# First attention of a fused decoder: weight splits on GpSimd, norms spread over the steps, a drain with its own order

## The reference, cut to what matters

```python
x = x + L0_attn(layernorm(x), wq, bq, wk, bk, wv, bv, wo, bo, ln_g, ln_b)
# inside: residual = h; h is normalised again, x = ln(h) * ln_g + ln_b
# q, k, v = x @ w.T + b, 16 heads of 128; rope(q), rope(k)
# attn = softmax(causal(q k' / sqrt(128))); o = attn v; return o @ wo.T + bo + residual
x = x + L0_xattn(layernorm(x), ctx, ctx, Wh, ...)     # V = einsum('bshd,hde->bshe', ctx, Wh)
```

## Time and profile before

| what | value |
|---|---|
| median of 3 runs | 999.65 us |
| profiled execution, its own time | 1000.2 us |
| its span | 998.4 us |
| TensorE busy over the span | 936.3 us (94%) |
| VectorE, ScalarE busy | 795.0 us (80%), 709.2 us (71%) |
| GpSimd busy | 359.3 us (36%) |
| mean granted TensorE clock | 0.99 |

### The profile page before, as it was taken

The page is one execution under the profiler, slowest core; times in us unless marked ns, Lnnn a source line. Parts: engine busy times, 40 slices in busy tenths (PEclk is TensorE's granted clock), DMA queues, the critical chain, the costliest instruction groups (busy, mean ns, idle before and its releaser), DMA issues. The chain is left out here.

```text
span 998.4 us, 19509 instructions
## 1 busy us (share of the span) xinstructions
PE 936.3 (94%) x6587; PEld 780.0 (78%) x6603; DVE 795.0 (80%) x1558; ACT 709.2 (71%) x1973; POOL 359.3 (36%) x323
## 2 busy tenths in 40 slices
PE   8789999999999999999969988788999989999998
PEld 4678888888889888898968876667778789875554
DVE  5999988888878797888827889889999754476885
ACT  5878877888778887777732347599999735448882
POOL 2343333433434334433300120166655310006882
PEclk9999999999999999999999997999999999999999
DMA  6423000000000000200125000000000000008762
GB/s 212 122 79 88 21 24 24 25 23 23 24 23 24 24 22 25 59 23 24 47 80 141 1 1 1 1 2 2 2 2 2 2 1 2 1 27 279 239 221 85
DMA packets 62084, 50.58 MB, mean 51 GB/s; under 512 B 18273, under 2 KB 53537, under 8 KB 61985
## 3 DMA queue, kind: packets, MB, share of 16 engines
q1 hardware_dynamic: 61984, 49.34, 16.7%
HBM read 36.74 MB, written 2.23 MB: 39 GB/s over the span
## 5 line engine op out<-in xcount | busy, mean ns | idle before, releaser
L391 POOL TENSOR_TENSOR roped_q<-roped_q,sin_q 128x512 f32<-128x512 f32 x64 | 82.9, 1295 | 261.9 <-DVE sin_q L553 261.9
L459 ACT ACTIVATE P<-banks,neg_max 128x128 f32<-128x128 f32 x256 | 90.4, 368 | 26.4 <-DVE neg_max L571 25.8
L391 POOL TENSOR_TENSOR roped_k<-roped_k,sin_k 128x512 f32<-128x512 f32 x64 | 82.9, 1296 | 45.5 <-DVE sin_k L553 45.5
L1745 ACT ACTIVATE win_P<-banks,win_neg_max 128x128 f32<-128x128 f32 x256 | 91.0, 382 | 4.9 <-DVE win_neg_max L1832 4.3
L499 ACT ACTIVATE oT_hi<-banks,bv_col 128x512 fp32r<-128x512 f32 x64 | 43.9, 687 | 67.5 <-PE banks L727 67.5
L1678 POOL TENSOR_TENSOR win_P<-win_P,win_inv 128x512 f32<-128x512 f32 x64 | 66.5, 1040 | 52.7 <-DVE win_inv L1837 52.6
L468 ACT ACTIVATE sin_q<-banks 64x512 f32<-64x512 f32 x128 | 75.9, 593 | 3.4 <-PE banks L37 1.1
L468 ACT ACTIVATE sin_k<-banks 64x512 f32<-64x512 f32 x128 | 75.8, 592 | 3.0 <-PE banks L37 0.8
L698 PE MATMUL banks<-roped_k,roped_q 128*128 128x128 f32 x512 | 68.3, 277 | 8.1 <-ACT banks L449 8.1
L683 PE MATMUL banks<-WO_lo,oT_hi 128*128 128x256 f32 x256 | 73.3, 286 | 2.4 <-DVE oT_lo L574 2.3
L552 DVE SCALAR_TENSOR_TENSOR roped_k<-banks,qk_bias,cos 128x512 f32<-128x512 f32 x64 | 48.0, 750 | 30.6 <-ACT sin_k L468 30.3
(11 more groups left out here) (439 smaller groups left out, 3093.0 us busy)
## 6 DMA issues: line engine op xcount, KB each, us to landing
PT<-blocks SPq DMA_DIRECT2D x630, 16.0 KB, 1.8
ret_V<-moe_gate_rows SPq DMA_DIRECT2D x16, 512.0 KB, 4.8
ctx<-moe_gate_rows SPq DMA_DIRECT2D x16, 512.0 KB, 5.5
X<-in_x SPq DMA_DIRECT2D x4, 512.0 KB, 6.8
stage<-in_wqT SPq DMA_DIRECT2D x4, 512.0 KB, 4.0
stage<-in_wvT SPq DMA_DIRECT2D x4, 512.0 KB, 6.6
stage<-in_woT SPq DMA_DIRECT2D x4, 512.0 KB, 4.9
ctx<-in_ctxT SPq DMA_DIRECT2D x4, 512.0 KB, 4.5
```

Source lines behind the costliest of these rows:

```text
L391: nc.gpsimd.tensor_tensor(roped[w][:, p, :], roped[w][:, p, :], sin_part[w][:], ALU.add).then_inc(roped_sum[w], 1)
L459: ins = nc.scalar.activation(P[:, :, i, :], SC[:, i * 128:(i + 1) * 128].rearrange("p (q n) -> p q n", n=Q), ACT.Exp, bias=neg_max[:, r % ...
L1745: ins = nc.scalar.activation(P[:, h % 2, s, i, :], SC[2 * (h % 2) + s][:, i * 128:(i + 1) * 128], ACT.Exp, bias=neg_max[:, h % 2, at:at + ...
```

## The change

VectorE no longer splits the weight items 4 to 15; GpSimd does, after its adds of step t, for the items of step t+1. The statistics of batches 4 to 15 move from steps 3 to 5 to six pairs in steps 3, 4, 16, 17, 21 and 23, and the one norm of 12 batches becomes three of 4 batches at the ends of steps 5, 18 and 25, each with its powers on GpSimd. The context tiles are loaded at SyncE's steps 53, 57, 61 and 63. The four last steps become a written sequence `drain()` per engine: the last two heads (62 and 63) are transposed on TensorE, the value products use three banks, and ScalarE and VectorE take them out in turn.

```diff
-        RET_BANKS = V_, XB, QK[0], QK[1]
+        RET_BANKS = V_, XB, QK[1]
+        STATS_AT = {3: (4, 5), 4: (6, 7), HEADS0: (8, 9), HEADS0 + 1: (10, 11), HEADS0 + 5: (12, 13), HEADS0 + 7: (14, 15)}
+        NORMS_AT = {5: 1, HEADS0 + 2: 2, HEADS0 + 9: 3}
+        POWERS_AT = NORMS_AT
-        LAST = STEPS - 1
+        LAST = STEPS - 2
+        LAST_BANKS = QK[0], SC
+        CTX_AT = {STEPS - 11: 0, STEPS - 7: 1, STEPS - 3: 2, STEPS - 1: 3}
...
                 def load_ctx(g):
-                    if g == 0:
-                        sp.wait_ge(v_projected, NG * HEADS0)
+                    sp.wait_ge(v_projected, (NG - 1) * HEADS0 + 4 * g + 4)
...
+                def split_weights(i):                      # GpSimd
+                    src, hi, lo = parts(i)
+                    pool.wait_ge(weights_rounded, i + 1)
+                    pool.wait_ge(weights_split, i)
+                    nc.gpsimd.tensor_tensor(lo, src, hi.bitcast(F32), ALU.subtract).then_inc(weights_split, 1)
...
                 for t in range(STEPS):
                     step(t, t % 2)
+                    if t + 1 < HEADS0:
+                        for i in split_at(t + 1):
+                            split_weights(i)
...
-                    if t == 6:
-                        powers(1)
+                    if t in POWERS_AT:
+                        powers(POWERS_AT[t])
...
+                def drain():                               # ScalarE
+                    exps(LAST)
+                    lay_mask(LAST)
+                    take_ret_V(0)
+                    take_PT(LAST)
+                    round_oT(LAST - 1)
+                    exps(LAST + 1)
+                    take_ret_V(2)
+                    round_oT(LAST)
+                    take_PT(LAST + 1)
+                    take_ret_V(4)
+                    take_ret_V(6)
+                    round_oT(LAST + 1)
...
-                    if g == 0 and r > 0:                   # VectorE
-                        for i in split_at(r):
-                            split_weights(i)
...
-                        if r in (3, 4, 5):
-                            group_stats(r - 2)
-                        if r == 6:
-                            both_norms(1)
...
+                    if s in STATS_AT:
+                        some_stats(STATS_AT[s])
+                    if s in NORMS_AT:
+                        both_norms(NORMS_AT[s])
...
+                def drain():                               # VectorE
+                    find_max(LAST)
+                    split_oT(LAST - 2)
+                    scale_last(LAST)
+                    take_ret_V(1)
+                    find_max(LAST + 1)
+                    split_oT(LAST - 1)
+                    scale_last(LAST + 1)
+                    take_ret_V(3)
+                    split_oT(LAST)
+                    take_ret_V(5)
+                    split_oT(LAST + 1)
+                    take_ret_V(7)
...
+                def drain():                               # TensorE
+                    last = lambda u: (u, u % HEADS0)
+                    retention_values(0)
+                    retention_values(1)
+                    out_project(*last(LAST - 2), NG - 1)
+                    score(LAST + 1, (LAST + 1) % 2)
+                    transpose_last(LAST)
+                    weigh(*last(LAST - 1))
+                    retention_values(2)
+                    retention_values(3)
+                    weigh(*last(LAST))
+                    out_project(*last(LAST - 1), NG - 1)
+                    transpose_last(LAST + 1)
+                    retention_values(4)
+                    weigh(*last(LAST + 1))
+                    out_project(*last(LAST), NG - 1)
+                    for p in (5, 6, 7):
+                        retention_values(p)
+                    out_project(*last(LAST + 1), NG - 1)
```

## The result

Six runs of the changed kernel have a median of 1004.2 us (1002.25 to 1005.92), six of the kernel before 999.56: the ratio is 1.0049, with a 95% interval of 1.0032 to 1.0066. The change costs half a per cent. The profiled execution took 1004.77 us by its own time, its span is 1002.7 (998.4 before).

What follows compares the result with a forecast made beforehand. VectorE and ScalarE's loop was taken to bound group 0, TensorE group 1, context waits the drain. +6.6 + 5.2 - 5.9 = +5.9 us on the median 999.65 gave 1005.5 us; range 995 to 1010, likeliest case alone 1002 to 1009.

Steps and rivals of the forecast that it cites:

- group 0: Steps 0 to 15: GpSimd's splits and the moved norm make TensorE start step 16 later by 6.6 us.
- group 1: From step 16: statistics and norms moved here make rounds exceed TensorE's steps, costing 5.2 us.
- the drain: Last four steps: context waits and half-clock value matmuls go, less new waits; gain 5.9 us.
- Collision: Group 0: GpSimd's 1024-column split shuts out VectorE's scaling until it ends; rounds 8.3 us, 8.7 with a batch; chance 0.58.
- Step 3: Group 0: two GpSimd splits, over the scaling and the q sine product, cost 2.1, less 1.2 and 0.67: +0.2 us.
- The norm's trap: Step 5: the norm's last two-input operation waits out GpSimd's split, +2.3 us, with 0 as the other end.
- The clock: Step 5: TensorE's clock may fall after idling some 4.5 us, adding 0 to 2 us outside the sum.
- bare round: Time between row maxima without added VectorE work: 7.14 us, winning back only 0.23 us a step.
- lateness: Row maximum's start minus TensorE's step start; beyond 1.53 us TensorE waits; forecast 1.3 at step 16.
- the rival that it gives nothing: Drain: the new order has its own waits and its gain is gone; 1011 us, chance 0.05.
- No collision: Group 0: GpSimd's split doesn't hold the scaling, and group 0 gains 4.3 us; 994 us in all, chance 0.27.
- Half a collision: Engines share the port at half speed, or the norm slips through; 999 to 1002 us, chance 0.10.

Runs made afterwards that it cites:

- halves: The changed kernel with each GpSimd weight split made as two instructions of 512 columns; 1001.49 us, ratio 1.0021.
- drain_gpsimd: The changed kernel with statistics and the one norm of 12 batches back in their old places, GpSimd still splitting; 1000.87 us, ratio 1.0005.
- drain_only: The kernel before with only the new drain and early context loads; splits on VectorE, statistics and norm in their old places; 992.24 us, ratio 0.9935.
- drain_spread: The changed kernel with the weight splits back on VectorE, statistics and norms still spread; 994.54 us, ratio 0.9955.
- extra1024: drain_only plus one useless GpSimd subtract of 1024 columns behind the k add in each of steps 16 to 59; 1044.61 us, ratio 1.0438.
- extra512: drain_only plus one useless GpSimd subtract of 512 columns behind the k add in each of steps 16 to 59; 1000.42 us, ratio 1.0003.
- extra256: drain_only plus one useless GpSimd subtract of 256 columns behind the k add in each of steps 16 to 59; 995.83 us, ratio 0.9963.
- beside: drain_only with the statistics and norms spread, but placed behind the output's low half, beside ScalarE's exponentials; 990.79 us, ratio 0.9908.

## Why the prediction was right

The forecast was 1005.5, the median is 1004.2, and the sign came from the mechanism that was named. No errors cancelled between the three terms: group 0 cost 5.9 for 6.6, group 1 4.35 for 5.2, and the drain gave 6.35 for 5.9, so each came out on the fast side of its forecast, and the sum is 4.2 in the starts (4.6 in the medians) for 5.9.

- **Collision.** Full exclusion, by 1024 columns in 2.4: measured 2.35 to 2.65. VectorE's scaling ends 0.56 after GpSimd (forecast 0.55), a round with a split takes 8.16 to 8.34 (8.3; steps 2, 4, 7 and 11), with a batch 8.65 to 8.67 (8.7).
- **Round by round,** after less before, measured and in brackets forecast: step 2 +0.94 (1.1), 3 -0.06 (0.2), 4 -0.24 (0), 5 +3.12 (3.4), 6 -2.02 (-2.0), 7 +0.74 (0.8), 8 to 10 +1.77 (1.95), 11 +1.00 (1.1), 12 +0.70 (0.8). The sum is 5.95 for 7.35, with each term a little below its forecast. Step 16 starts 5.9 later for 6.6.
- **Step 3** came out near its forecast by another way, which is luck. Two collisions had been forecast in it; there is one, the q sine product (1.49 for 0.74), and the scaling isn't caught (0.70, at 38.30). It starts 3.6 behind the maximum and not 2.5, because ScalarE's exponentials start late: WK's load is issued at 30.30, as soon as GpSimd's split of step 2 is done (28.84 in the kernel before), and ScalarE, which rounds that tile first, waits 2.2 for it. The prediction had held the later load against the block moves only, and not against ScalarE's rounding.
- **The norm's trap** was there, 2.22 for one instruction of four elements, in the place and for the reason given. halves and drain_gpsimd show that it hangs on a GpSimd instruction next to the norm, not on the change's own place for it.
- **The clock** was put at 0 to 2 us beside the sum. It did fall behind the gap of step 5: 12 output projections and 8 score matmuls ran in part at 1.2 GHz. No loss beyond the round is seen: rounds 6 and 7 are 7.14 and 8.34, the lengths of a bare round and of one with a split. VectorE and ScalarE, not TensorE, set them.
- **Group 1.** Rounds 16 to 19 were forecast as 7.79, 7.79, 9.1 and 8.4, and are 7.81, 7.79, 9.07 and 8.34. The loss is 4.35 for 5.2. Some 0.4 of the difference is the lateness that group 0 handed over, 0.91 instead of 1.3: steps 17 and 18 lose 0.2 for 0.6. The other 0.5 had been put on steps 22 to 24 and 30, where lateness stays at 1.48 or less, within the slack of 1.53, and nothing is lost.
- **The drain** gave 6.35 for 5.9, alone in drain_only 6.4, so the rival that it gives nothing falls.
- **The rivals.** No collision would have been drain_spread's or better (its splits cost 0.1 or less a round): 994.5, and the forecast for that case was 994. That it is the collision that separates the two is shown by drain_spread against the changed kernel, 9.7 us in the medians, 8.3 in the attention. Half a collision falls too: at half speed the scaling would lose at most its own 0.69, and it loses 1.19 (1.88 for 0.69).
- **What was off** stands in the expectations of the runs, not in the forecast: extra1024 came out 12 us above, extra512 5 to 8, extra256 3 to 4. The step that failed is the same: the round was taken for bare, with the scaling alone to be caught. In extra512 4.4 us of it lie behind the attention, in extra256 1.5.

## What to carry to other kernels

An engine that looks idle is no free engine if its instructions share a port with the one that sets the pace: before moving work to GpSimd, lay its start and end over the SBUF instructions of VectorE in the same round, and let the moved instruction end before they begin; cutting it in two won 3 of the 8 us or so that it had cost here, since each half caught something else. In a loop of two engines the length of an added piece says little and its place says nearly all: the same statistics and norms cost group 1 4.1 us behind the k products and nothing beside the exponentials. And one good part and two bad ones look like one small loss; taken one by one they were -6.4, +2.2 and +7.9.

## What the hardware showed

- Waiting goes both ways. GpSimd's subtract stood 1.0 behind VectorE's split of the input (2.29 for 1.29), and 0.5 behind the scaling in halves. The prediction's sum had only VectorE losing. The Trainium skill (SBUF — State Buffer, Who interferes with whom) says that whichever instruction starts first has the port for its whole length; the trace agrees in every row of an add or a subtract shown here. GpSimd's power is an exception, two points below.
- VectorE instructions with one SBUF input wait too: h_of 1.38 for 0.41, xn 1.01 for 0.41, L61 with four elements 1.19 for 0.17. One with PSUM for one of its two inputs does not: the low half of the output took 0.73 beside GpSimd's k add (88.84 in the changed kernel).
- GpSimd's power is long, 2.27 us for 12 elements a partition, but doesn't hold VectorE: beside the one that starts at 75.53 in drain_gpsimd, the normalised batch took 0.41 (75.60) and the scaling, with both inputs in SBUF, 0.69 (76.14). No run shows why.
- The stretch behind the attention, the same in all kernels, took 475.5 (beside) to 480.5 us (extra512); its granted clock was 0.97 in extra512 and 0.99 in drain_only. That is as much as many of the differences looked for here, so the parts are told by the starts in the attention and the medians only bear out their sign.
- The starts have a spread of their own. Five kernels have the same group 0 (before, drain_only and the three with an extra subtract) and start step 16 between 138.04 and 139.20. Most of this stands ahead of step 2's row maximum, which comes at 25.64 to 26.59; from there to the maximum of step 16 they agree within 0.25 (113.45 to 113.70). By that stretch group 0 costs 119.48 in the changed kernel, 120.55 in drain_gpsimd, 117.33 in halves, 112.05 in beside and 111.49 in drain_spread, and every sign given above holds.
